# One more wait in GpSimd's gather loop: the gathers of a chunk are issued after those of the preceding chunk have landed

## The reference

```
def _rel_layer(h, src, dst, etype, norm, V, comp, loop_w, bias, activation):
    c = comp[etype]
    m = 0
    for b in range(8):
        m = m + c[:, b, None] * (h @ V[b])[src]
    agg = segment_sum(m * norm, dst)
    out = agg + bias + h @ loop_w
    return relu(out) if activation else out

h = relu(layernorm(x));  x = x + rel_layer2(rel_layer1(h, ...), ...)
h = relu(layernorm(x));  x = x + gcn_conv(relu(gcn_conv(h, W1, b1)), W2, b2)
```

## Time and profile before

| | |
|---|---|
| median of 3 runs | 2128.14 us (2127.25 to 2131.23) |
| profiled execution | 2125.18 us, its span 2123.6 us |
| busy, share of the span | PE 85%, PEld 63%, DVE 56%, ACT 17%, POOL 68% |
| layer 0: TensorE's first and last chunk | 95.4 to about 1062 us |
| layer 1: TensorE's first and last chunk | 1105.7 to about 1968 us |
| granted TensorE clock, mean | 0.739 |

### The profile page before, as it was taken

The page is one execution under the profiler, slowest core; times in us unless marked ns, Lnnn a source line. Parts: engine busy times, 40 slices in busy tenths (PEclk is TensorE's granted clock), DMA queues, the critical chain, the costliest instruction groups (busy, mean ns, idle before and its releaser), DMA issues. The chain is left out here.

```text
span 2123.6 us, 38749 instructions
## 1 busy us (share of the span) xinstructions
PE 1806.7 (85%) x11730; PEld 1346.7 (63%) x11731; DVE 1190.5 (56%) x2013; ACT 360.4 (17%) x869; POOL 1453.1 (68%) x1573
## 2 busy tenths in 40 slices
PE   1398998989888888887849989889999899978798
PEld 1277777777666676766637766666666666655455
DVE  7565665656555554654267766666666756612433
ACT  2022222222222221222201101001010101101200
POOL 5777777777777777777567777777777777776000
PEclk8555555555555555555579989999999999979899
DMA  5233333232232223223222222223332232334363
GB/s 144 68 78 96 80 80 93 77 98 76 76 95 77 77 77 93 78 74 88 60 65 63 60 59 60 58 83 83 97 88 83 80 95 75 90 92 128 130 216 124
DMA packets 188885, 186.53 MB, mean 88 GB/s; under 512 B 109132, under 2 KB 161085, under 8 KB 188794
## 3 DMA queue, kind: packets, MB, share of 16 engines
q0 software_dynamic: 47232, 96.83, 17.1%
q1 hardware_dynamic: 133510, 84.47, 14.1%
q10 hardware_dynamic: 8052, 4.04, 0.7%
HBM read 159.75 MB, written 25.47 MB: 87 GB/s over the span
## 5 line engine op out<-in xcount | busy, mean ns | idle before, releaser
L765 POOL DMA_INDIRECT ring<-h_rows,rel_idx x1356 | 1305.5, 963 | 425.6 <-issue 394.8
L1124 PE MATMUL rel_ps_z<-rel_C,ring 128*128 128x56 f32 x3128 | 540.5, 346 | 79.7 <-DMA ring<-h_rows,rel_idx 79.2
L1124 PEld LDWEIGHTS rel_ps_z<-rel_C,ring 128*128 128x128 f32 x3128 | 524.8, 260 | 94.4 <-issue 90.4
L1083 PE MATMUL rel_ps_p<-rel_h_parts,rel_pick 128*128 128x384 bf16 x2200 | 391.8, 337 | 48.4 <-DVE rel_h_parts L900 22.0
L910 DVE TENSOR_TENSOR rel_pick<-rel_src_row,dve_bank 128x1664 bf16<-128x1664 int32 (+1 forms) x176 | 319.5, 1816 | 182.8 <-PE rel_ps_p L1083 180.2
L1083 PEld LDWEIGHTS rel_ps_p<-rel_h_parts,rel_pick 128*128 128x128 bf16 x2200 | 217.3, 101 | 200.6 <-issue 66.5
L1184 ACT ACTIVATE rel_ZT<-rel_ps_z 128x304 f32 x292 | 114.2, 426 | 1071.2 <-PE rel_ps_z L1124 1065.7
L874 DVE TENSOR_TENSOR rel_lo<-dve_bank,src_lo_table 128x1024 bf16<-128x1024 f32 x98 | 120.0, 1225 | 235.2 <-PE rel_ps_a L1033 234.8
L1174 ACT ACTIVATE rel_A<-rel_ps_a 128x500 f32 x292 | 165.6, 603 | 454.4 <-PE rel_ps_a L1041 419.9
L464 DVE TENSOR_SCALAR rel_onehot<-rel_types,type_id 100x1024 bf16<-100x1024 uint8 x196 | 141.6, 764 | 166.1 <-DMA rel_types<-edge_types 163.0
L552 PE MATMUL rel_ps_o<-V,rel_ZT 128*128 128x128 f32 x784 | 142.4, 356 | 65.4 <-issue 62.3
(11 more groups left out here) (206 smaller groups left out, 1282.9 us busy)
## 6 DMA issues: line engine op xcount, KB each, us to landing
ring<-h_rows,rel_idx POOLq DMA_INDIRECT x1356
A_slabs<-rel_A SPq DMA_DIRECT2D x25, 800.0 KB
A_slot<-A_slabs SPq DMA_DIRECT2D x25, 800.0 KB, 4.4
early_slot<-A_slabs SPq DMA_DIRECT2D x18, 896.0 KB, 6.1
rel_types<-edge_types SPq DMA_DIRECT2D x97, 100.0 KB
rel_src_row<-in_src_dram SPq DMA_DIRECT2D x88, 64.0 KB, 3.1
last_slot<-A_slabs SPq DMA_DIRECT2D x4, 512.0 KB, 6.1
ring<-h_rows,idx_table POOLq DMA_INDIRECT x120
```

Source lines behind the costliest of these rows:

```text
L765: g_.indirect_dma_start(ring[:, s * CHUNK + i, :], None, rows_in, bass.IndirectOffsetOnAxis(ap=idx[which][:, n:n + 1], axis=0)).then_inc(l ...
L1083: ins = m_.matmul(ps_p[s][:, 0:3 * P], pick[:, b, :], h_parts[:, b, :, :].rearrange("p c n -> p (c n)"), start=(b == 0), stop=(b == SRC_BL ...
L1124: ins = m_.matmul(bank(ps_z[s], NB)[:, :, bass.ds(at[i], TW)], ring[:, first + i, :], C[s][:, i, :, :], start=False, stop=(i == n - 1))
```

## The change

Two lines are added to `chunk`. They hold GpSimd also on the semaphore of the other parity, until it counts all chunks up to `c - 1`.

```
                 hold(pool, edges_done, c - (SLOTS_RING - 1))
                 landed = (ring_even, ring_odd)[s % 2]
                 hold(pool, landed, landings(m * (SLOTS_RING // 2) + s // 2, late))
+                before = (ring_even, ring_odd)[(s + 1) % 2]
+                hold(pool, before, landings(m * (SLOTS_RING // 2) + (s + 1) // 2, late and s > 0 or is_end))
                 if s in (0, 2, 4):
                     hold(pool, idx_ready, m * 3 + (s // 2 - 2))
```

## The result

The changed kernel takes 2554.57 us (median of 4 runs, 2550.32 to 2555.70), against 2128.76 us before (median of 4 runs): a ratio of 1.1995, 95% interval 1.1974 to 1.2016. That is 426 us slower; 348 were forecast. The time lies within the range, and the rival that was likeliest to add something (A) did not happen. But the sum came near by errors that partly cancel, and one of its three terms lies outside its own bounds.

The account below looks back on a forecast made before the run. GpSimd's fixed pace of gathers was taken to bound both relational layers. Ordinary landings, slow landings and index copies, 267 + 61 + 20 = 348 us, gave 2476 us, with a range of 2405 to 2565.

Parts of the forecast that it names:

- Rival A: In layer 1 TensorE's clock falls with more waiting until TensorE is the bound again: 97 us more, 2573; chance 0.10.
- Term 1: At chunk boundaries of both layers each added wait costs an ordinary landing: 1.51 us x 177 = 267 us.
- Term 2: In both layers GpSimd feels slow landings: 12 us in layer 0 and 49 in layer 1, bounds 0 and 122.
- Term 3: Index copies ahead of slots 0, 2 and 6 stand bare behind the wait: 20 us, bounds 0 and 20.
- Rival B: Gathers inside a chunk lose their 0.30 us pause once the queue is drained: 2131 or 2109 us; chance 0.03.
- Rival C: The added wait is hidden by the ring's stock or met at once: 2128 us; chance 0.03.

Follow-up runs that it names:

- the early waits: The added wait only in chunks 8 to 39 of layer 0, against the kernel before: 2208.85 us, ratio 1.0385.
- the free instructions: The changed kernel with the added wait asking for the chunk three back, so always met: 2126.83 us, ratio 0.9997.
- the store's move: The changed kernel with layer 0's 800 KB slab store issued one chunk later: 2519.79 us, ratio 1.1853.
- the run with the odd chunks: The changed kernel with the added wait before odd chunks only, in both layers: 2331.61 us, ratio 1.0953.

## Why the prediction was right, and where it was not

**The bound and the mechanism: right.** GpSimd's steady pace ends both layers. This is shown by the early waits (+83), by the free instructions (+0) and by the wait behind the second gather (+45).

**Term 1, the ordinary landing: too small.** 1.51 us per boundary were taken, 2.0 to 2.1 are measured (GpSimd idle 2.38 us less the 0.30 pause, at the row of 582.82; by the landing records 1.53 + 0.77 - 0.30 = 2.00 where no index wait follows). Its step that failed is "the difference between GpSimd's start after a semaphore and TensorE's, which no row shows", which I bounded by 0 and 0.30 and took as 0.15. It is 0.65 us, or 0.75 with an index wait behind; the upper bound was wrong as well. Over 177 boundaries the term is 354 to 368 us, for 267 taken and an upper bound of 294. The wait behind the first gather shows the restart by itself. That the time still lies within the range is luck: the range had room for 122 us of slow landings, and the term's excess used it. The pause between two free-running gathers was no measure for a restart.

**Term 2, slow landings: right in size only by chance.** 12 us in layer 0 and 49 in layer 1 were taken, from how often they were slow before. Measured are some 42 to 50 in layer 0 (what the store's move gave back; the difference of the 57 waits) and next to nothing in layer 1. The wait does not sample the slow landings at random: it ties TensorE, the stores that its work releases, and GpSimd's last gather into one rhythm. In layer 0 the store then meets the last gather of every fourth chunk, in layer 1 nearly nothing meets one. There SyncE loads slabs of 896 KB; this one, in the kernel before, goes out together with the last gather of chunk 78, the slow landing of the earlier trace rows:

```profile
1774.32 0.43 SPq L823 DMA_DIRECT2D early_slot<-A_slabs  x1
```

By the landing records 11 of the 16 slow landings of layer 1 before are at a chunk whose last gather had such a load from 4.5 us before its start to 1 us behind it; with the change 10 of the first 14 loads go out over 4 us behind the nearest last gather. No run moved these loads, so for layer 1 this is likely and not shown. That layer 1 came out at 192.3 for a forecast of 192 is therefore no success of the terms: some 45 too little in the first, about as much too much in the second. The whole miss of 78 us stands in layer 0 (233.8 for 156), about 44 of it from term 1 and 30 to 38 from slow landings.

**Term 3, the index copy: a little too large.** At the rows shown a copy makes the boundary 0.25 us longer, and it had cost 0.07 before: 0.18 more against the 0.30 taken, some 12 for 20 us over 66 copies.

**Rival A, TensorE's clock: did not happen.** It needed a mean clock under 0.75 (the late stretch's work per chunk is 8.1 us and not 8.2, so the point is 0.74) and few waits in layer 1. The windows of the changed kernel, in the columns of the earlier trace rows:

```profile
1480.00:1700.00 220.00, 181.83 (x1000) 122.38 (x1000) 112.93 (x167) 18.54 (x60) 133.73 (x147) 0.82 0.18 48
1720.00:2250.00 530.00, 459.93 (x2668) 309.28 (x2667) 275.95 (x419) 44.86 (x144) 320.36 (x354) 0.87 0.25 70
```

The clock did fall, from 0.92 and 0.97 to 0.82 and 0.87, and TensorE still waited 64 times, 138.5 us, for landings in layer 1:

```profile
PE rel_ps_z L1126 <- DMA ring<-h_rows,rel_idx: 138.5, 64, 7.5
```

So its direction was right and its point of decision was not reached. The rule of the Trainium skill (TensorE: Matmul & The Clock Gate, "HAM oscillation — how this bites in real kernels"), that each burst starts slow when the wait before it is long against the burst, did not decide here: the 64 waits are 2.2 us on average beside some 7 to 8 us of work in a chunk, and only some of them are long. The trace agrees with it for the longest: behind the four waits of 6.57 to 7.48 us in layer 1 the chunk's matmuls ran at the lower clock. Behind a short one they ran at the higher.

```profile
1556.21 1.99 PE L1126 MATMUL rel_ps_z<-rel_C,ring 128*128 128x56 f32 x16 [0.42 <-DMA ring<-h_rows,rel_idx]
...
2362.45 3.66 PE L1126 MATMUL rel_ps_z<-rel_C,ring 128*128 128x56 f32 x16 [6.60 <-DMA ring<-h_rows,rel_idx]
```

**Rival B, cheaper gathers from empty queues: did not happen.** Inside a chunk the pause stays 0.30 us, right behind a drained queue too (the rows at 1304.38 and 1305.62). The idle times of 2 us are still there (longest 2.2 and 2.3 us in the "issue" rows above), and the issue time of all gathers fell by only 8.5 us (1305.5 to 1297.0). **Rival C** fell with the chunks 8 to 39.

The Trainium skill's figure for a gather (DMA: Bandwidth & Descriptors, "Anatomy of one DMA — SWDGE (gpsimd) path", an estimate of 2.15 us) gave 0.90 us per boundary; measured are 2.0. From its start to its landing a gather takes 2.48 us here (0.95 + 1.53), 0.33 more than the estimate, and the restart of 0.77 is no part of that figure.

## What to carry to other kernels

A wait for a DMA just issued, put on the engine whose issue pace bounds the stage, costs its landing and the engine's restart at every use, 2.0 us here, whatever stock the consumer holds; placed two gathers later it cost a tenth of that here (45 us for 426), all of it from slow landings. Price a restart from a row in which that engine really stood on such a wait, not from the pause it has when it runs free. A wait can also lock the engines into one phase, so how often a transfer was slow before says little of after: look for what will be issued just ahead of the last transfer that the wait is for.

## What the runs showed of the hardware

- GpSimd's first gather starts 0.77 us after the landing that it was blocked on, TensorE's matmul 0.12 us after the same one (landing records; the rows at 582.01 and 582.66 of the run with the moved store show the 0.65 between them). With an index wait behind the blocked wait it is 0.87 us (the rows at 582.07 and 582.82 of the changed kernel, 0.75 apart), with an index copy 1.1. What makes up the 0.77 was not tried.
- A store of 800 KB issued 0.2 to 2.8 us ahead of a gather's start turned its landing from 1.55 into 3.5 to 4.4 us after the gather's end, 20 times in a row; issued 0.3 to 1.9 us behind the start, as in the run with the odd chunks, it left the landing at 1.7 us or less, 16 times.
- Gathers issue at 1.25 us each (0.95 and a pause of 0.30), whether the queues are drained or not.
